# Near rows of a cross network's second layer get a weight table of their own

## The reference, cut to what matters

```python
x0 = x                                   # r_x: 512 x 39 fields x 64
h = x
for W in (W0, W1):                       # 39 x 39 x 128 and 39 x 128 x 128
    h = jnp.einsum('bid,bjd,ijh->bhd', x0, h, W)
    outs.append(h)
out = jnp.concatenate(outs, axis=1).sum(axis=-1)   # 512 x 256
```

## Time and profile before

| what | us |
|---|---|
| median of three runs | 250.3 (250.0 to 250.98) |
| the profiled execution | 250.63 |
| its span, first to last instruction | 248.8 |
| TensorE matmul busy | 238.8 (96%) |
| VectorE busy | 178.0 (72%) |
| ScalarE busy | 167.8 (67%) |

### The profile page before, as it was taken

How to read it: one execution, slowest core, us unless ns; L and a number is a source line. 1 busy time by engine, 2 the same in 40 slices (tenths; PEclk the granted TensorE clock), 3 DMA queues, 4 the chain that set the end, 5 groups by cost and what they waited for, 6 DMA issues and landing times.

```text
span 248.8 us, 12083 instructions
## 1 busy us (share of the span) xinstructions
PE 238.8 (96%) x5578; PEld 203.0 (82%) x5578; DVE 178.0 (72%) x318; ACT 167.8 (67%) x309; POOL 0.6 (0%) x8
## 2 busy tenths in 40 slices
PE   1999999999999989999999999999999999999994
PEld 0577799968888878888888888888888888888993
DVE  1056999999958799699799779969969967700000
ACT  2489980042615458888887888888887888888300
POOL 0000000000000000000000000000000000000000
PEclk9999999999999999999999999999999999999999
DMA  5999100110101202522432252152252240110111
GB/s 177 418 396 403 69 0 7 16 22 36 57 3 54 56 9 26 167 56 25 137 104 18 41 190 30 30 171 59 26 149 86 25 114 22 16 25 18 11 25 30
DMA packets 15523, 20.66 MB, mean 83 GB/s; under 512 B 9424, under 2 KB 10352, under 8 KB 15088
## 3 DMA queue, kind: packets, MB, share of 16 engines
q1 hardware_dynamic: 15472, 19.89, 28.2%
HBM read 17.35 MB, written 0.52 MB: 72 GB/s over the span
## 4 chain that ended last, share of the span: by engine, by line
PE 77%; DVE 13%; SPq 4%; DMA 2%; ACT 2%; issue 1%; DVEq 0%
PE psum L537 34%; PE psum L518 22%; PE psum L494 12%; PE psum L477 7%; SPq L310 4%; PE psum L550 3%; DVE arena L377 3%; DVE arena L358 2%; DVE arena L361 2%; ACT arena L451 2%; DMA arena<-in_w 1%; DVE arena L398 1%; DVE arena L382 1%; DVE arena L402 1%; DMA arena<-arena 1%
## 5 line engine op out<-in xcount | busy, mean ns | idle before, releaser
L451 ACT COPY arena<-psum 64x460 f32<-64x460 f32 x256 | 137.6, 538 | 54.7 <-PE psum L518 51.7
L537 PEld LDWEIGHTS psum<-arena 128*64 128x64 f32 x1680 | 93.4, 137 | 10.5 <-issue 10.3
L537 PE MATMUL psum<-arena 128*64 128x128 f32 x1680 | 100.4, 274 | 0.0
L518 PE MATMUL psum<-arena 64*32 64x230 f32 x2048 | 57.4, 357 | 1.2 <-DVE arena L402 1.2
L358 DVE TENSOR_TENSOR arena<-arena 128x1600 f32<-128x1600 f32 x32 | 58.2, 1820 | 0.0
L361 DVE TENSOR_TENSOR arena<-arena 128x1520 f32<-128x1520 f32 x32 | 55.6, 1736 | 0.0
L494 PE MATMUL psum<-arena 128*32 128x128 f32 (+3 forms) x1194 | 48.9, 318 | 0.0
L494 PEld LDWEIGHTS psum<-arena 128*32 128x32 f32 x1194 | 43.2, 109 | 6.0 <-issue 2.3
L518 PEld LDWEIGHTS psum<-arena 64*32 64x32 f32 x2048 | 37.8, 106 | 12.5 <-issue 4.4
L477 PE MATMUL psum<-arena 128*32 128x230 f32 x512 | 27.9, 385 | 5.4 <-DMA arena<-in_w 5.4
L431 ACT COPY arena<-psum 64x460 f32<-64x460 f32 x44 | 25.9, 589 | 8.6 <-PE psum L477 8.0
(11 more groups left out here) (11 smaller groups left out, 11.2 us busy)
## 6 DMA issues: line engine op xcount, KB each, us to landing
arena<-in_x SPq DMA_DIRECT2D x32, 312.0 KB, 3.8
arena<-in_v_first SPq DMA_DIRECT2D x1, 1520.0 KB, 7.7
arena<-in_v_second SPq DMA_DIRECT2D x1, 1520.0 KB, 11.3
arena<-in_w SPq DMA_DIRECT2D x1, 1280.0 KB, 7.2
arena<-in_w_ones SPq DMA_DIRECT2D x2, 448.0 KB, 11.0
arena<-in_w SPq DMA_DIRECT2D x2, 320.0 KB, 3.5
arena<-in_w SPq DMA_DIRECT2D x1, 640.0 KB, 4.6
arena<-arena SPq DMA_DIRECT2D x24, 26.2 KB
```

The costliest lines, as they stand in the source:

```text
L451: done = nc.scalar.copy(view(s0[n % 2] + EXTRAS * q * B + 8 * in_batch + 4 * odd, (B, SLOTS), (2, 2), (1, 2), rows=(HALF * q, HALF * q + H ...
L518: done = nc.tensor.matmul(bank_view((COUPLES[couple(g)] + r) * BANK + m, (2, LIST), rows=(ROWS * c, ROWS * c + ROWS)), view(x0 + u % X_RIN ...
L537: nc.tensor.matmul(bank_view(at + HID, (1, HID), rows=(HALF * side, HALF * side + HALF)), view(s0[n % 2] + j * B, (1, B)), view(c0 + j * H ...
```

## The change

Only the 105 slots that are weighed one by one (`OWN`) get direct and mixed weights. The lists are 210 wide instead of 230, C is smaller by ten slots, and the tables AX and ZERO fall away (86 rows of V instead of 95). The extras' turns go: 27 turns hold the own slots, and turn 18 (`NEAR_TURN`) is new. It holds the 160 near rows: five strips of up to 32 rows, eight matmuls of 128 columns each, from a table `v_near` that is loaded in two halves and summed on VectorE; two copies take them out of the bank, to chunks of 128 and 32 rows. The two DMAs out of C go. The gather takes three pieces for the near rows instead of two. `mixed_order` writes one order over all turns, always the strip with the fewest columns so far, at most one turn ahead of the slowest. The weighing's parts are 28, 28, 28 and 21 matmuls instead of 27, 27, 27 and 24.

```diff
+EXTRAS = 10
+OWN = SLOTS - EXTRAS
...
-    names = [("A0", l) for l in H0] + [("AN", l) for l in H0] + [("AX", l) for l in N1]
-    names += [("B0", l) for l in H1] + [("BN", l) for l in H1] + [("BX", l) for l in N0] + [("ZERO", 0)]
+    names = [("A0", l) for l in H0] + [("AN", l) for l in H0]
+    names += [("B0", l) for l in H1] + [("BN", l) for l in H1] + [("BX", l) for l in N0]
...
-    if b == ONE:
-        return [(table["ZERO", 0], a - 20)]
     both = [(a, b)] if a == b else [(a, b), (b, a)]
-    if is_extra(which, pair):
-        return [(table["BX" if which else "AX", l], m) for l, m in both]
+    if which and a in N0:
+        return [(table["BX", l], m) for l, m in both]
...
-NEAR = [[(quarter, 24, 8, 0, EXTRAS)] for quarter in (0, 2)]
+NEAR = [[(0, 24, 8, 0, EXTRAS), (2, 24, 8, 0, 6)], [(2, 24, 8, 6, 4)]]
...
+def near_rows(pair_of):
+    seen, chunks = set(), []
+    for pieces in NEAR:
+        rows = []
+        for quarter, row, count, slot, slots in pieces:
+            for c in N1:
+                for a, b in pair_of[quarter][slot:slot + slots]:
+                    product = tuple(sorted((a, b, c)))
+                    rows.append(None if product in seen else product)
+                    seen.add(product)
+        chunks.append(rows)
+    return chunks
+IN_BANK = 4
+TURNS = -(-OWN // IN_BANK) + 1
+NEAR_TURN = 18
+NEAR_STRIPS = [(0, strip, strip) for strip in range(4)] + [(1, 0, 3)]
+def first_slot(k):
+    return EXTRAS + IN_BANK * (k - (k > NEAR_TURN))
+def own_slots(k):
+    return [] if k == NEAR_TURN else range(first_slot(k), min(first_slot(k) + IN_BANK, SLOTS))
+def mixed_order(pair_of):
+    waiting = [[] for _ in range(4)]
+    for quarter, steps in enumerate(waiting):
+        for k in range(TURNS):
+            if k == NEAR_TURN:
+                for i, (chunk, _, strip) in enumerate(NEAR_STRIPS):
+                    if strip == quarter:
+                        steps += [[k, V_ROWS + len(N1) * i + n, chunk, N1[n], 1] for n in range(len(N1))]
+                continue
+            of = [terms(quarter % 2, pair_of[quarter][j]) for j in own_slots(k)]
+            first = len(steps)
+            for t in range(2):
+                for place, some in enumerate(of):
+                    if t >= len(some):
+                        continue
+                    row, m = some[t]
+                    last = steps[-1] if len(steps) > first else None
+                    if last and last[1] == row and last[2] + last[4] == place and last[3] + last[4] == m:
+                        last[4] += 1
+                    else:
+                        steps.append([k, row, place, m, 1])
+    columns, order = [0] * 4, []
+    while any(waiting):
+        behind = min(steps[0][0] for steps in waiting if steps)
+        quarter = min((q for q in range(4) if waiting[q] and waiting[q][0][0] <= behind + 1), key=lambda q: columns[q])
+        k, row, place, m, count = waiting[quarter].pop(0)
+        order.append((k, quarter, row, place, m, count))
+        columns[quarter] += count
+    return order
...
-        c0 = take(SLOTS * HID)
+        c0 = take(OWN * HID)
...
-        u_raw0 = u0 + 2 * LIST
-        assert u_raw0 + 4 * LIST <= prod0
+        u_raw0 = u0 + 4 * OWN
+        assert u_raw0 + 8 * OWN <= prod0
...
-            return (view(c0 + 8 * i + odd, (HID, SLOTS), (4, 2), (2, 2), rows=(HALF * q, HALF * q + HALF)),
-                    bank_view(i % 4 * 2 * BANK + 2 * SLOTS * q, (2, SLOTS), (BANK, 2), (1, 2),
+            return (view(c0 + 8 * i + odd, (HID, OWN), (4, 2), (2, 2), rows=(HALF * q, HALF * q + HALF)),
+                    bank_view(i % 4 * 2 * BANK + 2 * OWN * q, (2, OWN), (BANK, 2), (1, 2),
...
+            for half, at in enumerate((v_near0, v_near_second0)):
+                sp.dma_start(view(at, (1, NEAR_WORDS)), v_near[half]).then_inc(near_loaded, 16)
...
-            sp.wait_ge(c_added, -(-EXTRAS // IN_BANK))
-            for i, pieces in enumerate(NEAR):
-                at = 0
-                for quarter, row, rows, slot, slots in pieces:
-                    first = ROWS * quarter + row
-                    sp.dma_start(view(c_near0 + i * HID, (1, HID), rows=(at, at + rows * slots)),
-                                 view(c0 + slot * HID, (HID, slots), (1, HID), rows=(first, first + rows)))\
-                        .then_inc(near_moved, 16)
...
+            dve.wait_ge(near_loaded, 32)
+            v = view(v_near0, (1, NEAR_WORDS))
+            add(v, v, view(v_near_second0, (1, NEAR_WORDS)), ALU.add).then_inc(near_ready, 1)
             dve.wait_ge(direct_copied, direct_by_act(DIRECT))
             dve.wait_ge(direct_moved, DIRECT // 3)
             dve.wait_ge(mask_ready, 1)
-            for k in range(MIXED):
-                slots = min(IN_BANK, SLOTS - IN_BANK * k)
-
-                masked = max(0, min(slots, FOREIGN[-1] + 1 - IN_BANK * k)) if IN_BANK * (k + 1) > FOREIGN[0] else 0
+            for k in range(TURNS):
                 dve.wait_ge(mixed_filled, k + 1)
-                if masked:
-                    c = view(c0 + k * BANK, (1, masked * HID))
-                    done = nc.vector.scalar_tensor_tensor(
-                        c, c, view(mask0, (1, 1)), bank_view(mixed_bank(k) * BANK, (1, masked * HID)), ALU.mult, ALU.add)
-                if masked < slots:
-                    c = view(c0 + k * BANK + masked * HID, (1, (slots - masked) * HID))
-                    done = add(c, c, bank_view(mixed_bank(k) * BANK + masked * HID, (1, (slots - masked) * HID)), ALU.add)
+                bank = mixed_bank(k) * BANK
+                if k == NEAR_TURN:
+                    for i, pieces in enumerate(NEAR):
+                        strips = [strip for chunk, _, strip in NEAR_STRIPS if chunk == i]
+                        source = (ROWS * strips[0], ROWS * strips[-1] + ROWS)
+                        done = nc.vector.tensor_copy(view(c_near0 + i * HID, (1, HID), rows=(0, height(pieces))),
+                                                     bank_view(bank + i * HID, (1, HID), rows=source))
+                else:
+                    words = len(own_slots(k)) * HID
+                    c, mixed_terms = view(c0 + (first_slot(k) - EXTRAS) * HID, (1, words)), bank_view(bank, (1, words))
+                    if first_slot(k) < FOREIGN[-1]:
+
+                        done = nc.vector.scalar_tensor_tensor(c, c, view(mask0, (1, 1)), mixed_terms, ALU.mult, ALU.add)
+                    else:
+                        done = add(c, c, mixed_terms, ALU.add)
...
+            act.wait_ge(near_ready, 1)
...
-                each = -(-(SLOTS - EXTRAS) // BATCH_UNITS)
+
+                each = 28
...
-                    pe.wait_ge(near_moved, 16 * sum(len(pieces) for pieces in NEAR))
...
+            order = mixed_order(PAIR_OF)
+            last_step = {step[0]: i for i, step in enumerate(order)}
+            banks_begun, quarters_begun = set(), set()
+            for i, (k, c, row, place, m, count) in enumerate(order):
+                if k not in banks_begun:
+                    mixed_bank_free(k)
+                    if k == NEAR_TURN:
+                        pe.wait_ge(near_ready, 1)
+                    banks_begun.add(k)
+                done = nc.tensor.matmul(
+                    bank_view(mixed_bank(k) * BANK + place * HID, (1, count * HID), rows=(ROWS * c, ROWS * c + ROWS)),
+                    view(v0 + row * ROWS, (1, ROWS)),
+                    view(w1_0 + m * PIECE, (PIECE, count), (PLACES * PIECE, PIECES), (1, PIECE)),
+                    start=(k, c) not in quarters_begun, stop=True, skip_group_check=True)
+                quarters_begun.add((k, c))
+                if i == last_step[k]:
+                    done.then_inc(mixed_filled, 1)
+                    if k in SUMS_BEHIND:
+                        sums(2 * SUMS_BEHIND[k])
+                        sums(2 * SUMS_BEHIND[k] + 1)
...
+    near = near_rows(pairs)
+    v_near = _np.zeros((2, hid, len(NEAR_STRIPS), len(N1), ROWS), f32)
+    for i, (chunk, part, _) in enumerate(NEAR_STRIPS):
+        for r, product in enumerate(near[chunk][ROWS * part:ROWS * part + ROWS]):
+            for m in set(product or ()):
+                a, b = (product[t] for t in range(3) if t != product.index(m))
+                v_near[0, :, i, m - N1[0], r] = w0[field(a), field(b)]
+                if a != b:
+                    v_near[1, :, i, m - N1[0], r] = w0[field(b), field(a)]
```

More of the change, by code:

```diff
@@ L82 @@
 V_ROWS = len(v_tables())
[L85 to L111, removed]
 ONES = [[(0, ONE - 8, 1, EXTRAS, 105), (1, 0, 20, 1, 1)], [(2, ONE - 8, 1, EXTRAS, 105), (1, 0, 20, 2, 1)],
@@ L127, in cin_kernel @@
 def cin_kernel(nc: bass.Bass, x: bass.AP, u_list: bass.AP, w1: bass.AP, v_first: bass.AP, v_second: bass.AP,
-               w0_ones: bass.AP, out: bass.AP):
+               w0_ones: bass.AP, v_near: bass.AP, out: bass.AP):
     P, ALL_PAIRS, _ = x.shape
@@ L211, in cin_kernel @@
         direct_moved = sem("direct_moved")
[L212 removed]
```

(38 more changed lines are left out.)

27 lines of the change are left out of this document (9 added, 18 removed).

## The result

The kernel after takes 256.77 us (median of 4 runs, 256.39 to 257.09) against 250.56 before on the same chip (4 runs): a ratio of 1.0249, interval 1.022 to 1.0277. The direction was forecast, the size was not: 2.0 us were predicted and 6.2 measured, outside the range of 250.6 to 253.3.

What follows compares the result with a forecast made beforehand. TensorE was taken to bound the kernel, except at three gates: two of VectorE's additions and the gather's issue. Terms 0.1 + 0.36 + 0.8 + 0.8 gave plus 2.0 us on 250.3: 252.3, range 250.6 to 253.3.

Steps and rivals of the forecast that it cites:

- Mixed stage behind it: Mixed stage after the first sums: 38, 46, 38 columns per strip between bursts, at 0.221 us each 8.41, 10.2, 8.41.
- The first addition: VectorE's first addition: at 42.85 instead of 43.58, a gain of 0.75 us.
- sums 1: Second burst of sums on TensorE, waiting for VectorE's additions: at 52.4 instead of 53.24, a gain of 0.85 us.
- the wait inside turn 15: Mixed stage: strip 1 reaches turn 15 early and waits for bank 3 until turn 11 is added, 0.45 us later.
- VectorE's 5.8 us: Before the main loop: additions of turns 25 to 27 and products, loop at 90.1 against 89.99, TensorE idle near 1.9.
- the direct stage: First TensorE stage, direct weights: operands of 210 instead of 230 words, done 2.2 us earlier, at 30.9.
- the first gate: Before the second burst of sums: TensorE, there near 50.6, waits for VectorE's additions, some 1.8 us idle.
- The slow first stretch: Direct stage's first 5.9 us, at half pace: length kept, 17.5 sets pass instead of 16.
- The last landing: End of the gather: 14 DMAs instead of 13 at 0.81 each, plus 0.8 us (0.7 to 0.9).
- Plus 0.36: Main loop: weighing parts of 28, 28, 28, 21 put three more matmuls before the last sums, plus 0.36 us.
- I take 0.1 each: Main loop: the new 32-row matmul shape costs 0.1 us in each of eight batches, 0.8 (0 to 1.4).
- TensorE loses more: Rival: idle stretches grow or TensorE runs slow afterwards, 255; or VectorE 1 us later, 253.3; chance 0.08.

Runs made afterwards that it cites:

- e4: Kernel before with only the order inside turns 21 to 25 changed, strip 1's five or six steps first in each turn: 255.61 us, one run.
- e1: Kernel after with its fifth near strip on column strip 1 instead of 3: 250.17 us (10 runs) against 250.54 of the kernel before, ratio 1.0013.
- e2: Kernel after with an order that finishes one turn before it begins the next: 250.32 us, one run.
- e3: Kernel after with strips allowed two turns ahead of the slowest instead of one: 251.69 us, one run.
- e5: Kernel before with only the first three of strip 1's steps put first in each of turns 21 to 25: 253.73 us, one run.
- e8: e1 with VectorE's products of unit 6 moved from behind turn 25 to behind turn 27: 248.79 us (12 runs) against 250.02, ratio 0.9945.
- e7: e1 with the weighing cut into 27, 27, 27 and 24 matmuls again: 250.88 us, one run.
- e10: e6 with the products of unit 6 moved behind turn 27, as in e8: 247.50 us (6 runs) against 249.92 of the kernel before, ratio 0.9902.
- e6: Kernel after with the near rows in two chunks of 80 rows, six near strips and 13 gather DMAs: 247.98 us, one run.
- e9: Kernel before with only the weighing cut into 28, 28, 28 and 21: 247.89 us (4 runs) against 249.92, ratio 0.9911.

## Why the prediction was wrong, step by step

**The step that failed** is in "Mixed stage behind it": "At 8.41/38 = 0.221 us per column: 8.41, 10.2, 8.41." I summed columns per strip and took it that strips work side by side whatever the order. The runs showed 8.90, 11.79 and 13.2: from turn 18 on the order holds runs of three to five steps of strip 1, and such a run stops the other strips until its last step but one starts (e4: 1.0 us a turn). It cost 1.6 in turns 16 to 20 and 4.7 in turns 21 to 25 (13.13 - 8.41), 6.3 together. e1 removes it with one digit, e2 and e3 with two other orders, and e4 makes it in a kernel that has no near turn. My text names the very fact that leads there, strip 3 the fullest, and draws the wrong thing from it. The Trainium skill (TensorE: Matmul & The Clock Gate, Part 2) says that matmuls stay in program order and only weight loads are pulled ahead; e4 (13.40 instead of 8.40) and e5 (11.2) agree but for one step, since in e4 another strip starts at 75.57 while the run's sixth step still waits. I had not weighed that against the step list.

That the direction came true is luck: e2, with the same load on every strip and no such run of strip 1, took 250.32, and e1 can't be told from the kernel before.

**Right in mechanism and size.** The first addition came at 42.33 (predicted 42.85), sums 1 at 51.86 (52.4), the wait inside turn 15 made 8.90 of 8.41 (8.86), and e2, at 8.40, shows that it goes with running ahead. Behind turn 25's filling VectorE's 5.8 us ended in a main loop at 96.08, 5.84 after 90.24, with TensorE idle for 1.87 (1.9). e8 shortens the way to that gate by 1.5. The 14 DMAs issued in 11.27 (11.3).

TensorE's timeline in the kernel after has these rows for the first two groups of sums, beside the earlier trace rows:

```profile
50.40 1.01 PE L543 MATMUL psum<-arena 64*32 64x230 f32 x32
51.86 1.01 PE L543 MATMUL psum<-arena 64*32 64x230 f32 x32 [0.45 <-DVE arena L437]
```

**Mis-sized, with little effect.** TensorE left the direct stage at 32.1, not 30.9, so it waited 0.45 at the first gate and not 1.8. Its timeline has two idle stretches in that stage, 0.32 and 0.69, for which the profile names no releaser. With the same direct stage, e1, e7 and e10 show one such stretch each (0.31, 0.96 and 0.69) and e2, e3, e6 and e8 none; e2 began the mixed stage at 30.61 and waited 2.11 at the gate. So they come and go from one execution to the next, and what makes them stays open. The slow first stretch, which I had kept at its length, was shorter in work lost: 88 records in 5.82 us, where 64 were measured before and 70 forecast. The last landing came 0.50 later, not 0.8: the last piece, 32 rows, landed in 1.88 instead of 2.17.

**Wrong, and hidden in the sum.** "Plus 0.36" for the parts of 28 has the wrong sign: e9 is 2.0 us faster with that edit alone. "I take 0.1 each" for the 32-row shape was too little: 0.35 a batch by e6, twice my upper end of 0.17. In the kernel after the two nearly cancel, so that the main loop is 0.36 shorter up to the last sums where my terms gave about 1.0 longer (0.36 and six times 0.1). The rule of the Trainium skill that was cited there (TensorEngine Tiling, Key Properties) holds in its direction: the row of TensorE's weight loads in the kernel after (first two lines; the third is from the kernel before) has an idle stretch of 0.17 just at the change of shape.

```profile
115.99 0.19 PEld L575 LDWEIGHTS psum<-arena 32*64 32x64 f32 x2 [0.17 <-issue]
116.35 0.74 PEld L543 LDWEIGHTS psum<-arena 64*32 64x32 f32 x36 [0.17 <-issue]
...
110.32 0.78 PEld L518 LDWEIGHTS psum<-arena 64*32 64x32 f32 x38 [0.17 <-ACT arena L451]
```

At the end of a batch there are two such gaps, one more than before. With parts of 27 that is all (0.15 by e7): of 24 matmuls and nine chunks the last one is alone on its half anyway. With parts of 28 the price is 0.35: there the ninth chunk has a partner if it has 80 rows, and 32 rows don't seem to run beside another chunk, which is argued and not shown.

**The rivals.** None of mine was what happened. "TensorE loses more" came nearest in size (253.3 and 255, where 256.77 was measured) and named other causes.

## What to carry to other kernels

When several strips of the array work side by side, look at the program order as TensorE gets it, not only at the sum of columns per strip: a greedy order with a bound on running ahead turns a small unevenness into runs of one strip, and a run keeps the others waiting until all but its last two steps are done. Count such runs from the step list before trusting a sum. Where matmuls alternate between two halves of the array, cut them so that the halves get equal shares, and try the cut alone.

## What the runs showed of the hardware that was not expected

TensorE's matmuls to one strip, put one behind another, hold up matmuls to free strips that stand behind them in the program: five runs with 38 columns in all cost 5.0 us (e4), five with 27 columns 2.8 (e5). One waiting step of a strip is looked past: in each of the five turns of e4 the other strips start together with the run's last step but one. The busy time of TensorE (13.13 of 13.13 us) and its granted clock (1.00, the level of 2.4 GHz) show nothing of it.

A mean granted clock under 1 needn't have cost a run any time. In e6, whose mean is 0.995, the clock is 1.00 from 228 us to the last matmul's end at 242.93 and 0.50 (the level of 1.2 GHz) from 243.8 to 246.2, when TensorE had nothing left to do. Two of e1's ten runs have a mean of 0.989 and 0.991 (252.43 and 252.42 us); no trace of them was kept, so what their clock cost, if anything, stays open.
